# Two more waits on POOL's indirect transfers in a three-layer graph network

## What is computed

```
gathered = edge_val[:, None] * x[edge_col]
support = segment_sum(gathered, edge_row, num_segments=N)
h = concatenate([x, support], axis=1);  out = relu(h @ W + b)         # layer 0
...
e = leaky_relu(xl[src] + xr[dst], 0.2)                                # twice, a GATv2 layer
score = einsum('ehc,hc->eh', e, att)
ex = exp(score - segment_max(score, dst)[dst])
alpha = ex / maximum(segment_sum(ex, dst)[dst], 1e-16)
x = x + gelu(segment_sum(alpha[:, :, None] * xl[src], dst) + b)
```

## Time and profile before

| | before |
|---|---|
| median of 3 runs | 2588.24 us (2587.32 to 2589.81) |
| the profiled execution: time, span | 2584.12 us, 2582.3 us |
| PE busy in the span | 2086.6 us (81%) |
| POOL busy | 1662.7 us (64%) |
| DVE busy, ACT busy | 1593.4 us (62%), 1056.8 us (41%) |
| scatters L670, 440 of them | 436.7 us, 993 ns each, and 139.7 us idle before them |
| gathers L1058, 880 of them | 849.0 us, 965 ns each, and 242.4 us idle before them |

### The profile page before, as it was taken

How to read it: one execution, slowest core, us unless ns; L and a number is a source line. 1 busy time by engine, 2 the same in 40 slices (tenths; PEclk the granted TensorE clock), 3 DMA queues, 4 the chain that set the end, 5 groups by cost and what they waited for, 6 DMA issues and landing times. The chain is left out here.

```text
span 2582.3 us, 31699 instructions
## 1 busy us (share of the span) xinstructions
PE 2086.6 (81%) x7770; PEld 1439.5 (56%) x7770; DVE 1593.4 (62%) x3202; ACT 1056.8 (41%) x2798; POOL 1662.7 (64%) x1810
## 2 busy tenths in 40 slices
PE   0656666665499989799999999969699999999975
PEld 0444444444377765466666666645466666666654
DVE  8312111111266666488888888877488888888876
ACT  0233333333000013355555555544355555555543
POOL 3377777777400004788888888836788888888832
PEclk9776778778799999899999999989899999999987
DMA  3355353434499842544444444431444444444443
GB/s 95 83 123 118 120 117 120 114 119 118 124 267 265 264 126 77 132 113 112 113 126 111 112 113 113 108 65 47 123 110 114 112 115 113 114 111 112 113 78 100
DMA packets 208623, 311.81 MB, mean 121 GB/s; under 512 B 33396, under 2 KB 167542, under 8 KB 208471
## 3 DMA queue, kind: packets, MB, share of 16 engines
q0 software_dynamic: 64512, 171.82, 24.7%
q1 hardware_dynamic: 143799, 138.05, 21.1%
q10 hardware_dynamic: 160, 0.20, 0.0%
HBM read 243.75 MB, written 72.66 MB: 123 GB/s over the span
## 5 line engine op out<-in xcount | busy, mean ns | idle before, releaser
L1058 POOL DMA_INDIRECT gath<-gather_table,SRCI x880 | 849.0, 965 | 242.4 <-issue 210.4
L1108 PE MATMUL p_sums<-gath,OH 128*128 128x272 f32 x1760 | 476.6, 410 | 63.2 <-DVE gath L1015 29.1
L670 POOL DMA_INDIRECT rows_by_src<-gath,node x440 | 436.7, 993 | 139.7 <-issue 115.8
L615 PE MATMUL p_expd<-X,OHT 128*128 x880 | 301.6, 504 | 220.6 <-DVE OHT L581 220.5
L1077 PE MATMUL p_expd<-gath,ident 128*128 128x512 f32 x880 | 427.5, 609 | 31.9 <-DMA gath<-gather_table,SRCI 31.5
L1108 PEld LDWEIGHTS p_sums<-gath,OH 128*128 128x128 f32 x1760 | 323.2, 193 | 189.7 <-issue 86.6
L1081 PE MATMUL p_expd<-node,OHT 128*128 x1760 | 417.6, 380 | 0.0
L1081 PEld LDWEIGHTS p_expd<-node,OHT 128*128 128x128 f32 x1760 | 336.4, 191 | 142.0 <-issue 107.4
L615 PEld LDWEIGHTS p_expd<-X,OHT 128*128 128x128 f32 x880 | 210.6, 250 | 300.9 <-issue 264.1
L1136 DVE SCALAR_TENSOR_TENSOR work<-p_expd,VEC 128x512 f32<-128x512 f32 x440 | 282.2, 682 | 136.8 <-PE p_expd L1081 135.8
L648 ACT ACTIVATE gath<-p_expd,node 128x256 f32<-128x256 f32 x440 | 172.7, 476 | 387.7 <-DVE gath L584 336.8
(11 more groups left out here) (282 smaller groups left out, 2163.0 us busy)
## 6 DMA issues: line engine op xcount, KB each, us to landing
gath<-rows_by_src SPq DMA_DIRECT2D x122, 514.0 KB, 4.5
LBC<-local_rows SPq DMA_DIRECT2D x330, 128.0 KB, 3.1
gath<-gather_table,SRCI POOLq DMA_INDIRECT x880, 3.0
rows_by_src<-gath,node POOLq DMA_INDIRECT x440, 3.5
gather_table<-gath SPq DMA_DIRECT2D x50, 132.0 KB, 1.7
node<-gather_table SPq DMA_DIRECT2D x2, 3200.0 KB, 11.9
X<-in_x SPq DMA_DIRECT2D x1, 3072.0 KB
x<-X SPq DMA_DIRECT2D x5, 512.0 KB, 3.0
```

The costliest lines, as they stand in the source:

```text
L615: ins = pe.matmul(expd[q % 2][:, g // 2, (g % 2) * D:(g % 2 + 1) * D], OHT[:, q % 2, g * P:(g + 1) * P], Xv[:, bass.ds(tiles[g // 2], 1), ...
L670: pool.indirect_dma_start(sup_d[:, :], bass.IndirectOffsetOnAxis(POSI[:, i:i + 1], 0), U[:, q % 4, g, :], None, bounds_check=EP - 1, oob_i ...
L1058: pool.indirect_dma_start(ROWS[:, i % (RING * G), 0:XW], None, tab_d[:, :], bass.IndirectOffsetOnAxis(SRCI[:, i:i + 1], 0)).then_inc(gathe ...
L1108: ins = pe.matmul(sums[k][:, 0:RW], OH[:, a % 2, g, :], slots(a, g, g + 1)[:, 0, :], start=(g % 2 == 0), stop=(g % 2 == 1))
```

## The change

In the scatter stage POOL waits, from group 4 on, also until PE has expanded group q+2 (`exp_ready` at q+3, at most NG). In each pass the gathers 3 to 11 wait until PE has expanded group q-3 (`expanded` at q-2).

```
                 def _(pool):
                     for q in range(NG):
                         pool.wait_ge(u_ready, q + 1)
+                        if q >= 4:
+                            pool.wait_ge(exp_ready, min(q + 3, NG))
                         pool.nop(nofuse=True)
                         for g in range(G):
...
                         def gather(q):
                             if q >= RING:
                                 pool.wait_ge(summed, 2 * (q - RING + 1))
+                            elif q >= 3:
+                                pool.wait_ge(expanded, q - 2)
                             pool.nop(nofuse=True)
                             for g in range(G):
```

## The result

The changed kernel takes 2597.60 us in the median of 12 runs (2591.78 to 2602.26); the kernel before, measured beside it, 2586.84 us (12 runs, 2583.72 to 2589.81). The ratio is 1.0041, 95% interval 1.0033 to 1.0049: slower by 10.8 us, where 11.0 were forecast. The profiled execution took 2594.36 us.

A forecast was written before the change was run, and what follows sets the result against it. POOL was taken to bound the scatter stage and both passes; four late waits, 3.20 + 2.29 + 2.33 + 3.21 = 11.0 us, on the median of 2588.24 gave 2599 us, range 2591 to 2606.

The forecast's parts named there:

- POOL bounds the stages: Scatter stage and passes: POOL is full, so a microsecond it loses there is given back nowhere and lengthens the kernel.
- Four places, and no other: Only scatter groups 6 and 22 and gather 11 of each pass cost time, 11.0 us together; other waits cost nothing.
- Group 6: Scatter stage: its wait for expansion 8, late behind DVE's resets, costs 3.20 us.
- gather 11: Each pass: its wait for expansion 8, late behind the sum of group 0, costs 2.33 us in the first, 3.21 in the second.
- Group 22: Scatter stage: its wait for expansion 24, late behind DVE's reduction of the lows, costs 2.29 us.
- the shift from group 6 moves both sides alike: Scatter stage, group 22: the earlier delay shifts expansion 24 and POOL's start equally, so the cost stays 2.29 us.
- The second pass: Gather 11 of the second pass waits for expansion 8 and costs 3.21 us.
- the full-clock rival: TensorE at full clock at all four late places: they cost 2.9 us in sum, kernel 2591 us; chance 0.07.
- Release to first transfer: At a new wait, POOL's first transfer starts 0.97 us after the expansion releases it.
- The clock: TensorE is at half clock again after idling at all four late places, so the sum stays 11.0 us.
- Faster: Rival: the slow transfer after POOL's multiplication (1.20 us, not 0.98) speeds up, 12 us over both passes; 2579 us; chance 0.04.
- the 103 cost nothing: Scatter stage: 103 of 106 new waits have 1.28 us or more between expansion end and POOL's start, so cost nothing.

The follow-up runs named there:

- four only: The kernel before with only the new waits at scatter groups 6 and 22 and gather 11 of each pass; 1.0022 on chip 13, 1.0007 on chip 12.
- all but four: The changed kernel without its waits at scatter groups 6 and 22 and at gather 11 of both passes; 0.9830 on chip 13, 0.9827 on chip 12.
- POOL weighs less: The kernel before, no new waits; in the passes one tile of every second group moved from POOL's multiplication to DVE's; 1.0262 on chip 9.
- three ahead: The changed kernel with scatter group q waiting for expansion q+3 instead of q+2, and no new waits in the passes; 1.0049 on chip 9.

## Why the prediction was right, and how far

**POOL bounds the stages.** Right on the first chip, to a part of the loss. In the passes 1.6 of 2.08 and 2.0 of 1.92 us came through to the length of the pass, in the scatter stage 4.7 of 6.05. The last was not in the working: the 440 transfers of the scatter stage were busy for 435.3 us where it had been 436.7, 1.4 us less.

**Four places, and no other.** Right: 120 waits found their mark reached, group 7 with its slack of 0.0 as well. That the four carry the whole loss rests on the trace of the first chip; neither "four only" nor "all but four" ran on a chip of that sort.

**The terms.** The sum was right, 11.0 against 10.05. Two terms were near. Group 6 was put at 3.20 and cost 2.57; gather 11 at 2.33 and 2.08 in the first pass. Group 22 was put at 2.29 and cost 3.48: expansion 24 waited 8.21 us for `OHT` 24 instead of 4.19 in the earlier trace rows, so the step that mis-sized it is "the shift from group 6 moves both sides alike". The second pass was put at 3.21 and cost 1.92: its sum 0 took 3.60 us where the earlier trace rows have 3.97, and the first four matmuls of expansion 8 behind it 1.88 us where they had taken 2.60, so these twelve took 1.1 us less. The granted clock in the three stretches of 2 us from there was 0.55, 0.60 and 1.00 (from 1876) where before had 0.50, 0.50 and 0.59 (from 1868); that is the full-clock rival, in part and at one place. The two errors, +1.2 and -1.3, cancelled; that the sum hit so closely is luck to that extent.

**Release to first transfer.** Taken as 0.97 us from the earlier trace rows, after an idle of 19 us. At the four places it was 0.81 in the scatter stage (140.19 to 141.00, 226.31 to 227.12) and 0.72 in the passes (1097.33 to 1098.05, 1883.59 to 1884.31) from the start of the other released engine. Together that is 0.8 us, most of the difference between 11.0 and 10.05.

**The readings.** Two were a little off, and neither moved the sum: 14.6 of POOL's 105.2 us of idle time in the earlier trace rows were ended by PE's sums, so "never stands still for anybody" is too strong, and the upper end of the range adds up to 2605, not 2606.

**The clock.** Expansions 8 and 24 were slow again, as said (ACT's release at 226.31 is 3.8 us after expansion 24 began at 222.50).

**The rivals.** On the first chip none. "Faster" was given 0.04 for a mechanism that did not act: the transfer after a multiplication still takes 1.18 us. On chip 12 the change is faster, and on chips 13 and 9 kernels near to it are, by a mechanism that none of the rivals had: late increments. The prediction speaks of the kernel's time as if it belonged to the kernel alone; the step "the 103 cost nothing" holds on the first chip, and on the others those waits gain 46 to 50 us, more than four times what the late ones cost anywhere.

**What is shown and what is argued.** Shown: PE's increments reach ACT, DVE and POOL together, up to 33 us late, on chips 9, 12 and 13 and not on the first or on number 0; those of DVE and ACT aren't late where they are recorded. In before and in the changed kernel the time is lost where POOL issues transfers without a multiplication between; but the increments can be late elsewhere too, as in the passes of "POOL weighs less". Waits that break POOL's row win back 16.3 and 14.5 us of the 25.7 and 24.5 of the two fills and about 18 us in the scatter stage (chip 12). Argued only: that it is the density of POOL's own transfers that holds up PE's increments; the on-time increments of "three ahead" speak for it. Not settled: whether a pause without a wait would do, how long it must be, and what differs between the chips. One rival is untested. On the slower sort a trace holds less than half as many semaphore updates (17406 against 37215 for before), so the recording of them loses something there, and every execution in this document came with a recorded span and clock. Whether the recording has a part in the delay, no run tells.

## What to carry to other kernels

A wait on the engine that bounds a stage costs exactly what it comes too late by, so lay both times side by side for every turn, look first at the turns in front of which some other engine has an extra piece of work, and cost the rest at nothing only for the chip whose trace you read. Where one engine can run far ahead with indirect transfers, time both forms on more than one chip: a wait that holds it two or three groups back cost 0.4% here on one chip and gained 1.6% on another. And an experiment on another chip than the first is to be compared stage by stage: the ratio of "three ahead" hid a loss of the expected size behind one of the kernel before. The version to try first is the one without the four late waits: 0.983 on chips 12 and 13, which on chip 12 can't be told from the whole change; on the first sort of chip it wasn't timed, and nothing in the trace there speaks for a cost.

## What the runs showed of the hardware that was not expected

The same program, with the same durations of each transfer (966 ns a gather, 0.99 us a scatter), takes 2587 to 2588 us on the first chip and on number 0, and 2727 to 2733 us on three others, 5.5% more; the difference is 92 us in the scatter stage and 25 us in the fill of each pass. On the slower ones the message that an expansion is done came 11 and 33 us late while POOL issued 40 gathers in a row, and 2.3 to 5.1 us after POOL stopped in the three cases followed here (another came in the midst of the row). That PE's increment leaves PE at the end of the work is what the Trainium skill says too ("Perfetto Trace Analysis", "Tensor Engine Instruction (MATMUL, LD_WEIGHTS)": once the results are acknowledged, the update is sent and spreads to all engines, and the profile's end of a matmul is an estimate). The trace of the first chip agrees, with 0.04 us between; on chip 12 the update itself was recorded up to 33 us late, and the engines that waited started 0.02 to 0.09 us after the record, so the delay stands before the update and not in its spreading. The estimated end is not the reason, since PE had begun its next expansion.

A wait that does bind at a POOL transfer costs 0.7 to 0.8 us from the release of a neighbour engine to POOL's start. And 26 memsets of one column on POOL take 0.83 us together, 32 ns each, though each is listed with 109 to 126 ns.
